# A transformer stack on one core: queries and keys of a head pair as one 1024-column tile in two PSUM banks

## What is computed

```python
qkv = x @ Wqkv                                    # 16 heads of 64, 128 -> 3 * 1024
q = l2norm(q) * qs;  k = l2norm(k) * ksc
q = q * cos * scale + rotate_half(q) * sin * scale
k = k * cos * inv + rotate_half(k) * sin * inv    # inv = 1 / scale
# windows of 32 tokens, each looking at itself and the window before it
sim = einsum('bhwie,bhwje->bhwij', bq, bk2) * 8.0
attn = softmax(where(mask, -max, sim))
out = einsum('bhwij,bhwje->bhwie', attn, bv2) @ Wo
```

## Time and profile before

| | |
|---|---|
| three runs, median | 3368.71 us (3358.27 to 3374.22) |
| the profiled execution, span from first to last instruction | 3373.6 us, which is 0.6 us under the slowest of the three runs |
| VectorE (DVE) busy | 2981.4 us, 88% |
| TensorE (PE) busy | 2905.4 us, 86% |
| GpSimd (POOL) busy | 2425.2 us, 72% |
| ScalarE (ACT) busy | 2061.4 us, 61% |
| mean granted TensorE clock | 0.938 of full |

### The profile page before, as it was taken

The page is one execution under the profiler, slowest core; times in us unless marked ns, Lnnn a source line. Parts: engine busy times, 40 slices in busy tenths (PEclk is TensorE's granted clock), DMA queues, the critical chain, the costliest instruction groups (busy, mean ns, idle before and its releaser), DMA issues. The chain is left out here.

```text
span 3373.6 us, 132100 instructions
## 1 busy us (share of the span) xinstructions
PE 2905.4 (86%) x57914; PEld 1846.3 (55%) x57914; DVE 2981.4 (88%) x4200; ACT 2061.4 (61%) x3820; POOL 2425.2 (72%) x1679
## 2 busy tenths in 40 slices
PE   5788889989989899987767788998999988999987
PEld 3455555655655555653323455565566655565653
DVE  6789899999999899896898878989999989899994
ACT  3466566666666665664764456666666666566663
POOL 3678777787787687774454667778788787787773
PEclk8899999999999999998887889999999999999998
DMA  5233332333333333320001333333343333333330
GB/s 140 65 83 73 82 91 68 89 90 72 86 92 71 84 85 71 83 72 28 7 7 44 80 72 79 75 87 86 75 97 76 90 84 72 81 94 71 86 76 14
DMA packets 114726, 250.85 MB, mean 74 GB/s; under 512 B 27244, under 2 KB 60648, under 8 KB 114152
## 3 DMA queue, kind: packets, MB, share of 16 engines
q1 hardware_dynamic: 114152, 242.40, 30.3%
HBM read 37.82 MB, written 3.15 MB: 12 GB/s over the span
## 5 line engine op out<-in xcount | busy, mean ns | idle before, releaser
L1085 ACT ACTIVATE squares<-general 128x512 f32<-128x512 f32 x768 | 453.9, 597 | 720.8 <-PE general L658 712.2
L1279 POOL TENSOR_TENSOR probs<-probs,row_sum 128x1024 f32<-128x1024 f32 x192 | 365.3, 1903 | 426.3 <-DVE row_sum L957 425.5
L1259 POOL TENSOR_TENSOR q_ring<-q_ring,partner 128x512 f32<-128x512 f32 x384 | 491.1, 1279 | 216.6 <-DMA partner<-sines 216.3
L868 DVE SCALAR_TENSOR_TENSOR sines<-general,vec,consts 128x512 f32<-128x512 f32 x768 | 560.7, 730 | 68.4 <-ACT squares L1085 65.5
L1259 POOL TENSOR_TENSOR k_ring<-k_ring,partner 128x512 f32<-128x512 f32 x384 | 490.8, 1278 | 0.0
L692 PE MATMUL general<-probs_t,v_buf 32*64 32x64 f32 x24576 | 339.4, 236 | 158.3 <-issue 87.0
L656 PE MATMUL general<-xs_hi,wqkv_lo 128*128 128x512 f32 x768 | 457.3, 595 | 15.8 <-DVE xs_lo L897 7.6
L692 PEld LDWEIGHTS general<-probs_t,v_buf 32*64 32x64 f32 x24576 | 305.6, 135 | 248.8 <-issue 241.7
L1273 POOL TENSOR_TENSOR probs<-probs,q_scale 128x1024 f32<-128x1024 f32 x192 | 365.3, 1903 | 15.1
L668 PE MATMUL general<-att,wo 128*128 128x512 f32 x768 | 370.4, 627 | 6.5 <-ACT att L1155 5.2
L719 PE MATMUL general<-k_ring,q_ring 64*32 64x64 f32 (+1 forms) x24576 | 294.2, 224 | 88.4 <-issue 53.5
(11 more groups left out here) (232 smaller groups left out, 6348.2 us busy)
## 6 DMA issues: line engine op xcount, KB each, us to landing
partner<-sines SPq DMA_DIRECT2D x1536, 128.0 KB, 2.3
wqkv_raw<-in_wqkv SPq DMA_DIRECT2D x80, 208.0 KB, 2.7
wo<-in_wo SPq DMA_DIRECT2D x12, 512.0 KB, 5.1
w<-in_w SPq DMA_DIRECT2D x12, 341.0 KB, 3.2
base_dram<-x SPq DMA_DIRECT2D x8, 256.0 KB, 2.4
att<-in_wqkv SPq DMA_DIRECT2D x2, 1024.0 KB, 6.1
sines<-base_dram SPq DMA_DIRECT2D x8, 256.0 KB, 4.0
w<-in_w SPq DMA_DIRECT2D x12, 128.0 KB
```

The costliest lines, as they stand in the source:

```text
L868: e.scalar_tensor_tensor(out=by_seq(sines[:, i % 2, which, :]), in0=g, scalar=scale, in1=both(tables[:, 2 * which + 1, :]), op0=ALU.mult, ...
L1085: e.activation(squares[:, (2 * p + which) % 4, :], general_of(("proj", k, n, p, which))[:, :], ACT.Square).then_inc(S[f"squared_{side}"], 1)
L1259: e.tensor_tensor(y, y, partner[:, i % 2, which, :], ALU.add).then_inc(S[f"rotated_{side}"], 1)
L1279: e.tensor_tensor(y, y, spread_keys(row_sum[:, i % 2, :]), ALU.mult).then_inc(S["probs_done"], 1)
```

## The change

- Queries and keys of a pair get two neighbouring banks, under one semaphore. `Banks.use` takes a width; if two do not fit before the end of the ring, it goes on at bank 0. An item now takes 51 entries.
- All six matmuls of the projection stand at the head of the step; nothing of it stands behind the scores. ScalarE squares the 1024 columns in one operation, VectorE makes the sines in one and the cosines in one, GpSimd adds in one.
- The layer's scales are multiplied into the tables once per layer and stack (`dve_tables`, two operations of 512 columns, 24 in all), so that `scalar_tensor_tensor` becomes `tensor_tensor`.
- The mask of two banks is written in one operation, and the scores of both sequences are scaled in one.
- To make room, `inv_norm` shares memory with `k_inv`, and the scan block's weights are loaded at the end of the first stack into `wqkv_raw` and no longer at its start.

With two banks under one semaphore, a bank is free when the wide operation on both is done. The values of an even step now wait in two of their four banks for that step's `cos` of queries and keys, where the entry falls so.

```diff
-    def use(self, key, sem, value):
-        at = self.next
-        self.next = (at + 1) % self.banks
+    def use(self, key, sem, value, width=1):
+        at = self.next if self.next + width <= self.banks else 0
+        self.next = (at + width) % self.banks
+        taken = range(at, at + width)
+        self.of[key], self.before[key] = at, [self.last[i] for i in taken if i in self.last]
...
-                self.use(("proj", k, n, p, 0), "cos_q", (g + n) * PAIRS + p + 1)
+                self.use(("proj", k, n, p), "cos", (g + n) * PAIRS + p + 1, 2)
...
-                for seq in range(CHUNK_SEQS):
-                    self.use(("scores", k, n, group, seq), "k_norms_off", ((g + n) * GROUPS + group) * 2 + seq + 1)
+                self.use(("scores", k, n, group), "k_norms_off", (g + n) * GROUPS + group + 1, CHUNK_SEQS)
...
-            if st.now:
-                n, p = st.now
-                self.use(("proj", k, n, p, 1), "cos_k", (g + n) * PAIRS + p + 1)
...
-            if k == 0:
-                e.dma_start(mw[:, :, :], mw_in.rearrange("m d n -> d m n")).then_inc(S["m_loaded"], 16)
...
+            if k == 0:
+                w.wait_ge(S["wqkv_lo"], DEPTH * PAIRS)
+                e.dma_start(mw, mw_in.rearrange("m d n -> d m n")).then_inc(S["m_loaded"], 16)
...
-            w.wait_ge(S["sin_q"], i + 1)
-            w.wait_ge(S["sin_k"], i + 1)
+            w.wait_ge(S["sin"], i + 1)
...
+            pe_bank(w, ("proj", k, n, p))
...
+            for which in range(2):
+                g, cut = two_of(("proj", k, n, p))[:, which * COLS:(which + 1) * COLS], slice(which * P, (which + 1) * P)
+                e.matmul(g, wqkv_lo[:, p, cut], xs_hi[:, r, :], start=True, stop=False)
+                e.matmul(g, wqkv_hi[:, p, cut], xs_lo[:, r, :], start=False, stop=False)
+                done = e.matmul(g, wqkv_hi[:, p, cut], xs_hi[:, r, :], start=False, stop=True)
+            done.then_inc(S["proj"], 1)
...
+        def dve_tables(e, w, k, layer):
+            w.wait_ge(S["vec_loaded"], 16)
+            w.wait_ge(S["cos"], (k * ITEMS + layer * CHUNKS) * PAIRS)
+            for which in range(2):
+                e.tensor_scalar(layer_tables[:, which, :, :], tables[:, which, :, :], vcol(layer, V_QS + which), None, ALU.mult)\
+                    .then_inc(S["tables_scaled"], 1)
...
-            e.scalar_tensor_tensor(out=by_seq(sines[:, i % 2, which, :]), in0=g, scalar=scale, in1=both(tables[:, 2 * which + 1, :]),
-                                   op0=ALU.mult, op1=ALU.mult).then_inc(S[f"sin_{side}"], 1)
+            e.tensor_tensor(by_side(sines[:, i % 2, :, :]), g, layer_table(1), ALU.mult).then_inc(S["sin"], 1)
...
-            e.scalar_tensor_tensor(out=by_seq(qk_ring[which][:, slot_of(n, p), :]), in0=g, scalar=scale,
-                                   in1=both(tables[:, 2 * which, :]), op0=ALU.mult, op1=ALU.mult).then_inc(S[f"cos_{side}"], 1)
+            e.tensor_tensor(by_side(qk_ring[:, slot_of(n, p), :, :]), g, layer_table(0), ALU.mult).then_inc(S["cos"], 1)
...
-            for seq in range(CHUNK_SEQS):
-                start = k_inv[:, seq * SEQ:seq * SEQ + 1]
-                keys = bass.AP(start.tensor, start.offset, [list(start.ap[0]), [WIN, NWIN], [1, 2 * WIN]])
-                y = probs[:, i % PROBS, seq * COLS:(seq + 1) * COLS]
-                e.tensor_tensor(cube(y), cube(general_of(("scores", k, n, group, seq))[:, :]), keys, ALU.mult).then_inc(S["k_norms_off"], 1)
+            start = k_inv[:, 0:1]
+            keys = bass.AP(start.tensor, start.offset, [list(start.ap[0]), [WIN, ITEM_WINS], [1, 2 * WIN]])
+            e.tensor_tensor(cube(probs[:, i % PROBS, :]), cube(two_of(("scores", k, n, group))), keys, ALU.mult).then_inc(S["k_norms_off"], 1)
...
                 if st.now:
-                    dve_rotate(e, w, k, *st.now, 0)
+                    dve_sin(e, w, k, *st.now)
+                    dve_cos(e, w, k, *st.now)
...
-                if st.now:
-                    dve_rotate(e, w, k, *st.now, 1)
...
+                for sem, value in BANKS.free(key):
+                    w.wait_ge(S[sem], value)
+                e.activation(two_of(key).rearrange("p (s c) -> p s c", s=CHUNK_SEQS),
+                             mask_bf[:, :].unsqueeze(1).broadcast_to([P, CHUNK_SEQS, COLS]), ACT.Copy).then_inc(S["mask_set"], 1)
...
                 if st.now:
-                    act_square(e, w, k, *st.now, 0)
+                    act_square(e, w, k, *st.now)
```

More of the change, by code:

```diff
@@ L429, in macaron_kernel @@
         base_dram = nc.dram_tensor("base_dram", [P, TOKENS], F32).ap()
-        general = [bank(f"general{i}") for i in range(POOL_BANKS)]
-        sums = bank("sums")
-        SIDE = ("q", "k")
+        ring = banks("general", POOL_BANKS)
+        general = [ring[:, i * COLS:(i + 1) * COLS] for i in range(POOL_BANKS)]
+        sums = banks("sums", 1)
         recast = att[:, 0:5, :].rearrange("p a c -> p (a c)")
-        stage_v = qk_ring[0][:, 0:4, :].rearrange("p r (h d) -> p (r h) d", d=P)
+        stage_v = qk_ring[:, 0:2, :, :].rearrange("p r w (h d) -> p (r w h) d", d=P)
         stage_out = v_buf[:, 0, 0:NWIN, :].rearrange("p w (h d) -> p (w h) d", d=P)
@@ L500, in general_of, with two_of @@
             return general[BANKS.index(key)]
+        def two_of(key):
+            at = BANKS.index(key)
+            return ring[:, at * COLS:(at + 2) * COLS]
         SHIFTED, count = {}, 0
@@ L781, in tensor_stack @@
                 if st.now:
-                    pe_project(e, w, k, *st.now, 0)
+                    pe_project(e, w, k, *st.now)
                 if st.spread:
```

151 lines of the change are left out of this document (71 added, 80 removed).

## The result

Four runs of the changed kernel gave 3590.67 to 3606.41 us, median **3597.31 us**, against a median of 3370.97 us (3358.27 to 3374.22) of the kernel before, which has a fourth run by now. The ratio is **1.069** (95% interval 1.066 to 1.073). The profiled execution has a span of 3590.4 us, 216.8 more than the 3373.6 of before. The change is slower; the forecast said faster.

A forecast was written before the change was run, and what follows sets the result against it. VectorE was taken as the bound, TensorE and ScalarE close behind. From 3373.6 us, -125 + 2 + 78 + 45 - 30 = -30 gave 3344; 4 off for the wait of L904 gave 3340 us, range 3245 to 3430.

The forecast's parts named there:

- VectorE's work: Wide sines and cosines save 131 us, scores 10, less the tables' cost: together 125 us less work on VectorE.
- steps 1, 4, 5: The keys' operations no longer cover ScalarE's mask and square, so booked savings are lost and waits grow: plus 78 us.
- even steps: The values wait 0.97 us longer for the wide cosines, using up TensorE's slack in steps 2, 4, 6: plus 45 us.
- exp: Exp no longer stands behind the keys' square and projection: 30 us off VectorE's wait of 41.0.
- I cost it at nothing: GpSimd's two additions of 1.28 us become one of 2.4 to 2.56; booked at zero, at most 38 us either way.
- VectorE is the bound: VectorE is the busiest engine, with TensorE and ScalarE close behind and tied to it by banks.
- sign of error: Wrong if sines wait for squares no more, the steady clock falls under 0.94, or a wide product's record is 1.4 us.
- The second: Rival: TensorE becomes late in even steps and runs at half clock; slower, 3417 to 3455 us; chance 0.28.
- theory A: Explanation formed after the result, not in the prediction: VectorE stands behind long GpSimd instructions.
- The third: Rival: a wide operation over two banks is no cheaper than two, 1.31 us instead of 1.14; 3422 us; chance 0.07.
- The first: Rival: the hand-offs are covered and VectorE's saved work counts in full; 3249 us; chance 0.17.
- the fourth: Rival: everything cancels, with larger losses in steps 1, 4, 5 and slack costing 60 us; 3377 us; chance 0.18.

The follow-up runs named there:

- b_all_pieces: The kernel before with all of GpSimd's additions and passes over the scores cut into pieces of 256 columns; ratio 0.999.
- a_all_pieces: The changed kernel with GpSimd's addition and its three passes over the scores cut into pieces of 256 columns in every step; 3462.13 us, ratio 1.026.
- b_tables: The kernel before with the scales in layer tables, narrow products and the changed kernel's use of memory; 3368.76 us, ratio 1.002.
- b_pieces: The kernel before with GpSimd's two passes over the scores in step 1 cut into four pieces of 256 columns; ratio 0.996.

## Why the prediction was wrong

The prediction's sum can be set against a pair of spans in which the meeting with GpSimd is small on both sides, `b_all_pieces` (3374.4) and `a_all_pieces` (3456.5), whose five untouched operations take 149.6 and 152.6 us:

| term | forecast | measured | by |
|---|---|---|---|
| VectorE's work | -125 | -120 | 2924.6 to 2804.6 busy |
| idle time of VectorE: steps 1, 4, 5, even steps, exp, weights (78 + 45 - 30 - 4 + 2) | +91 | +202 | 449.8 to 651.9 |
| standing behind GpSimd | 0 | +134 | 3456.5 to 3590.4; nothing in the kernel before (3374.4 and 3373.6) |
| sum | -34 | +216 | span 3373.6 to 3590.4: 216.8 |

Of the 134 us: VectorE is busy 211.5 us longer in the changed kernel than with the pieces (189.0 in the five operations, 20.7 in the tables), and 77.6 of that come out of its idle time. In the kernel before, the pieces take 57 us of busy time away, and its idle time grows by as much. Of the 250 us between forecast and measured sum, then, 134 are the GpSimd term, 111 the hand-offs and 5 the work; without the first the change would still have been 82 us slower.

**The step that failed first is "GpSimd": "I cost it at nothing".** Its bound of 38 us either way priced a late addition in 384 steps, as if only those who need its result could suffer. The rows for the true price lay in the kernel before: L924, a subtraction of 128 columns, took 1862 ns on average where its neighbour L913 of the same size took 385, and L897's mean of 902 ns stood beside the 0.68 of the earlier trace rows. The prediction had only the latter before it, one record that happened to begin (808.02) in a gap of GpSimd's work, just behind this line of the kernel before (its end is 807.91), and read no group of those operations:

```profile
806.63 1.28 POOL L1259 TENSOR_TENSOR k_ring<-k_ring,partner 128x512 f32<-128x512 f32 x1
```

Twenty of the 48 records of L897 began while a GpSimd instruction ran, and took 1.21 us in the mean. The tables, booked "at up to 0.65, plus 16 us", took 1607 ns each, 37.6 us; those that met no GpSimd instruction took 0.48.

**The second step is "VectorE is the bound".** `b_tables` took 50 us of work from it and the time stayed; `b_pieces` took 59 and gave 0.4%; both together took 115 for 0.5%. TensorE is within 2% of it, and an engine that runs ahead stands in the next wait; that the two bound the time by turns fits this, but no run shows it directly. Idle time of VectorE is what grows: 392.2 us before, then 416.0, 411.5 and 484.5. The prediction counted saved work in full and every loss as a correction to it.

**The third is the size of the hand-offs, +91 for +202.** In the steady part of `b_all_pieces` and then `a_all_pieces`, the mean distance from a step's first sine to the next one's, for steps 0 to 7, is (to 0.1, which the choice of the stretch moves) 9.7, 8.4, 8.9, 5.8, 8.3, 6.1, 8.2, 5.9 us and then 10.1, 9.1, 8.2, 5.4, 9.9, 6.6, 8.6, 5.8. Steps 2 and 3 gain what was booked or more. Step 5 was forecast at 6.3 and has 6.6; step 1 loses 0.7. Step 4 loses 1.6, and is the largest: VectorE's waits for TensorE grow there, by 0.6 us for the feed-forward's last product (L995), 0.5 for the projected values and 0.3 for the scores, and that for squares by 0.4. TensorE waits for the cosines and has more projection ahead of this work; that this is what makes it late is argued from the order and not shown by a run. The prediction gave step 4 the chain of ScalarE alone, and put TensorE's lateness into a flat 45 us. Step 6, forecast at 7.4, has 8.6 in the mean and 7.7 in the median: the forecast had read one undisturbed item, whose 7.70 us lie at the low end of the kernel before (mean 8.3).

What was right: that steps 1, 4 and 5 lose, by waits for squares among others; the widths (1.14 forecast, 1.13 and 1.14 measured; squares at 1.02 for 1.03; 1212 ns for the scores), the wait for L668 (62.7 to 16.9), exp (41.0 to 9.4, for "near 10"), step 5's chain (6.6 us against 6.3), and the direction of the wait of sines for squares, 254.0 where 180 to 220 was given. Busy time down by 100 to 130 us was not right: it rose by 34.7. The prediction's own sign of error fired: the clock of the steady stretches is 0.92 and 0.91, under 0.94.

**The rivals.** The second had the right side and one of the mechanisms: TensorE waits 254.1 us for the ring, and behind such a wait its values run at 1.2 GHz (0.50, above). Its price, up to 3455, is close to the 3462 that the changed kernel has with GpSimd in pieces, but that may be luck, as no run measures the clock's part; without theory A it could not reach 3597. The third fell: a wide operation costs 1.13 us and not 1.31. The first fell with the result, and the fourth with it. The estimate of 1.19 us for a wide operation by the Trainium skill (VectorE: DVE Perf Modes, "The TRN2 errata") lies over the 1.13 to 1.14 from start to start, and under the record of 1.21. With its saving of 92 us for 131 the sum would have come to some 3379 us, no gain, and still over 200 us too low.

Open: why the order costs as much in half of the steps as in all, though the busy part of it is the standing behind GpSimd, and how much of the time is the clock's fall itself (0.96 and 0.97 in the steady stretches of `b_all_pieces`, 0.94 in those of `a_all_pieces`) and how much the waits that go with it. Neither was told apart.

## What to carry to other kernels

Before you merge two operations, ask who stands still while the merged one runs: here GpSimd's addition in one cost VectorE 57 us of busy time in one kernel and 78 in the other, and a mean far above an operation's shortest record, or above a neighbour's of the same size, is the sign to look for. Where two engines are within a few per cent of each other, a saving on one can be worth next to nothing by itself (50 us of work gave none here), while a result that comes later costs; price the first result as well as the sum of work. GpSimd work beside a busy VectorE is worth trying in short pieces, even where the pieces take longer in all: it gave 3.8% in the changed kernel, though no more than 0.4% in the kernel before.

## What the runs showed of the hardware

- A VectorE instruction that meets a running GpSimd instruction stands until that one ends, then does its work: L914 0.68 us alone, 2.79 behind an addition of 2.39; L924 1862 ns beside passes of 1.90 us, 655 beside pieces of 0.62. Subtractions of two SBUF tiles, a cast and a `tensor_scalar` of one did so; reciprocals (953 ns), transposes (711), row maxima (1161) and products out of PSUM (1212 ns at 1024 columns) kept their times in the kernels before and after.
- One VectorE or ScalarE instruction reads 1024 columns over two PSUM banks, and no seam shows: 1.13 us from start to start for a product (two of 512 cost 1.19), 1.02 for a square (two cost 1.19).
- GpSimd adds 1024 columns of two tiles in 2.39 us, 512 in 1.28 and 256 in 0.75; with one operand repeated along the columns, 1024 take 1.90 and 256 take 0.62.
- Behind a wait of 4.18 us TensorE ran 128 small matmuls at a granted clock of 0.50 in 2.29 us; at 1.00 they took 1.55.
